# The last combination of a two-expert layer: every second pair of sequences moved from VectorE, ScalarE and GpSimd to TensorE

## What is computed

```python
x = x + jnp.tanh(g_xattn[0]) * _L0_xattn_ref(ctx_1024, ctx_1024, _layernorm(x, axis=-1), L0_xattn_w_out, L0_xattn_b_out)
x = x + jnp.tanh(g_ffn[0]) * _L0_ffn_ref(_layernorm(x, axis=-1), ...)
# the last lines of _L0_ffn_ref
ye = jnp.einsum('ecf,efd->ecd', h, W2) + b2[:, None, :]
out = ye[idx1, pos1] * (w1 * keep1)[:, None] + ye[idx2, pos2] * (w2 * keep2)[:, None]
```

## Time and profile before

| | before |
|---|---|
| median of 3 runs | 418.43 us (417.49 to 420.23) |
| the profiled execution, in all | 418.9 us |
| its span | 416.8 us |
| TensorE busy | 314.3 us (75%) |
| VectorE busy | 273.1 us (66%) |
| ScalarE busy | 220.2 us (53%) |
| GpSimd busy | 220.8 us (53%) |
| moved by DMA | 33.85 MB, mean 81 GB/s |

### The profile page before, as it was taken

How to read it: one execution, slowest core, us unless ns; L and a number is a source line. 1 busy time by engine, 2 the same in 40 slices (tenths; PEclk the granted TensorE clock), 3 DMA queues, 4 the chain that set the end, 5 groups by cost and what they waited for, 6 DMA issues and landing times.

```text
span 416.8 us, 13745 instructions
## 1 busy us (share of the span) xinstructions
PE 314.3 (75%) x3993; PEld 255.5 (61%) x3994; DVE 273.1 (66%) x1084; ACT 220.2 (53%) x656; POOL 220.8 (53%) x367
## 2 busy tenths in 40 slices
PE   1689987877878877878752079999999999999300
PEld 1356655545545545555441079999999998999300
DVE  4758987787787887876467425555555555555286
ACT  2478866665576566665430135555555555555131
POOL 2413366756656656656667105555555554555352
PEclk9999999999999999999995569999999999999755
DMA  7933321212212110000001212222222222221196
GB/s 204 304 113 108 114 90 65 78 40 77 76 43 80 61 57 29 21 28 29 25 29 47 71 44 64 64 64 63 63 64 65 63 67 56 61 60 56 55 355 197
DMA packets 40157, 33.85 MB, mean 81 GB/s; under 512 B 4998, under 2 KB 32936, under 8 KB 40112
## 3 DMA queue, kind: packets, MB, share of 16 engines
q1 hardware_dynamic: 35216, 24.58, 20.2%
q0 software_dynamic: 4320, 8.43, 6.3%
q10 hardware_dynamic: 576, 0.26, 0.3%
HBM read 17.95 MB, written 15.77 MB: 81 GB/s over the span
## 4 chain that ended last, share of the span: by engine, by line
PE 39%; issue 26%; ACT 13%; DVE 5%; DMA 4%; SPq 2%; another core or an unknown queue 1%; DVEq 1%; POOL 0%; ACTq 0%; POOLq 0%
PE main_scores L704 15%; PE main_scores L690 15%; ACT qT L520 5%; ACT probs L527 5%; PE max_scores L681 2%; DVE x_all L913 2%; DVE x_all L917 2%; PE main_scores L623 1%; DMA choice_rows<-y_s,dest 1%; PE mixed L598 1%; ACT oS L532 1%; DMA yc<-choice_rows 1%; ACT xn2T L512 1%; DMA expert_rows<-pad 1%
## 5 line engine op out<-in xcount | busy, mean ns | idle before, releaser
L474 POOL DMA_INDIRECT choice_rows<-y_s,dest x71 | 78.8, 1109 | 81.6 <-DVE y_s L894 46.5
L545 ACT ACTIVATE hT<-main_scores,ex_cur 128x128 f32<-128x128 f32 x284 | 81.2, 369 | 70.5 <-PE main_scores L690 69.7
L772 DVE TENSOR_REDUCE negmax<-max_scores 128x8 bf16<-128x1024 f32 x64 | 77.9, 1217 | 32.6 <-remote 21.7
L527 ACT ACTIVATE probs<-main_scores 128x1024 f32<-128x1024 f32 x64 | 62.0, 1021 | 45.7 <-issue 43.2
L690 PE MATMUL main_scores<-xtT,ex_cur 128*128 128x128 f32 x568 | 78.5, 282 | 1.5 <-DVE xtT L886 1.5
L704 PE MATMUL main_scores<-w_sb,hT 128*128 x568 | 79.2, 283 | 0.4 <-ACT hT L545 0.4
L431 POOL DMA_INDIRECT expert_rows<-xrow,slot_i x64 | 64.2, 1003 | 16.8 <-issue 16.1
L690 PEld LDWEIGHTS main_scores<-xtT,ex_cur 128*128 128x128 f32 x568 | 70.6, 195 | 3.3 <-DVE xtT L886 1.9
L704 PEld LDWEIGHTS main_scores<-w_sb,hT 128*128 128x128 f32 x568 | 69.6, 193 | 1.7 <-issue 0.6
L884 DVE COPY ex_cur<-ex_sb 128x644 f32 x71 | 35.3, 497 | 49.4 <-issue 35.4
L458 POOL TENSOR_TENSOR rstd<-ve,neg_half 128x1 f32<-128x1 f32 x32 | 17.7, 554 | 53.2 <-DVE ve L757 52.9
(11 more groups left out here) (132 smaller groups left out, 473.2 us busy)
## 6 DMA issues: line engine op xcount, KB each, us to landing
xt<-expert_rows SPq DMA_DIRECT2D x71, 64.5 KB
choice_rows<-zeros SPq DMA_DIRECT2D x16, 256.0 KB
yc<-choice_rows SPq DMA_DIRECT2D x16, 256.0 KB, 5.4
ex_sb<-in_L_ffn_W_dram SPq DMA_DIRECT2D x4, 512.0 KB, 4.7
w_sb<-in_L_ffn_W_dram SPq DMA_DIRECT2D x4, 512.0 KB, 4.4
out_dram<-x_all SPq DMA_DIRECT2D x8, 256.0 KB, 3.8
x_all<-in_x_dram SPq DMA_DIRECT2D x5, 384.0 KB, 6.2
ctx_all<-in_ctx_dram SPq DMA_DIRECT2D x5, 384.0 KB, 6.2
```

The source lines that it names most:

```text
L474: nc.gpsimd.indirect_dma_start(y_dram, bass.IndirectOffsetOnAxis(ap=dest[:, v, :], axis=0), y_s[:, v, :], None, bounds_check=last_row, oob ...
L527: nc.scalar.activation(probs[:, b % 2, 2 * g:2 * g + 2, :].rearrange("p g k -> p (g k)"), E_ALL[:, 1024 * g:1024 * g + 1024], ACT.Exp, sca ...
L545: last = nc.scalar.activation(hT[:, v % 2, c, :], H_BANK[v % 2][:, c * P:c * P + P], ACT.Gelu, bias=ex_cur[:, v, FF + D + c:FF + D + c + 1])
L772: V.tensor_reduce(negmax[:, m % 3, 2 * h:2 * h + 2, 0:J], S_ALL[:, :].rearrange("p (g j k) -> p g j k", g=2, j=J), AX.X, ALU.max, negate=T ...
```

## The change

In each chunk VectorE now takes two sequences instead of three (32 instructions instead of 48), and the other two go to TensorE. For each chunk TensorE adds up in one PSUM bank: x of both sequences (256 columns, times the identity), and for each of them its two answers, each multiplied by a 128x128 diagonal matrix with the gate of row s at place (s, s). ScalarE copies the 256 columns of the sum back into `x_all`. The 32 diagonal matrices (`diag`) are made by GpSimd from the identity and `gw`, after its last scatter to `expert_rows` and ahead of its first scatter to `choice_rows`. For that the six steps of `gw` move on VectorE from the end of stage 2 to its beginning. What ScalarE and GpSimd did in the last combination is gone.

```diff
+        diag = sb("diag", [P, K, B // 2, P])
...
             for k in range(NC):
-                sp.wait_ge(fin_done, (CH - 1) * (k + 1))
-                sp.wait_ge(pool_fin_done, k + 1)
+                sp.wait_ge(fin_done, CH // 2 * (k + 1))
+                sp.wait_ge(act_fin_done, k + 1)
...
+            pool.wait_ge(gates_done, 1)
+            for k in range(NC):
+                for c in range(K):
+                    for u in range(CH // 2):
+                        q = CH * k + CH // 2 + u
+                        last = nc.gpsimd.tensor_scalar(diag[:, c, CH // 2 * k + u, :], ident[:, :], gw[:, c, q:q + 1], None, ALU.mult)
+            last.then_inc(diag_done, 1)
             pool.wait_ge(zeroed, 16 * NZ)
...
-                    nc.gpsimd.tensor_tensor(x_all[:, cols(s)], x_all[:, cols(s)], yc[:, c, s, :],
-                                            ALU.add).then_inc(pool_fin_done if c else pool_first_added, 1)
...
-            act.wait_ge(gates_done, 1)
             for k in range(NC):
-                s = CH * k + CH - 1
-                act.wait_ge(yc_loaded[k], 16 * K)
-                for c in range(K):
-                    nc.scalar.activation(yc[:, c, s, :], yc[:, c, s, :], ACT.Copy, scale=gw[:, c, s:s + 1]).then_inc(scaled, 1)
+                s = CH * k + CH // 2
+                act.wait_ge(sum_psum, k + 1)
+                nc.scalar.copy(x_all[:, s * D:(s + CH // 2) * D], E_BANK[k % 4][:, 0:CH // 2 * D]).then_inc(act_fin_done, 1)
...
+            pe.wait_ge(diag_done, 1)
+            for v in (2, 3):
+                pe.wait_ge(y_ready[v], NI + (v < NV))
+            for k in range(NC):
+                s = CH * k + CH // 2
+                wait(pe, act_fin_done, k - 3)
+                nc.tensor.matmul(E_BANK[k % 4][:, 0:CH // 2 * D], ident[:, :], x_all[:, s * D:(s + CH // 2) * D],
+                                 start=True, stop=False, skip_group_check=True)
+                pe.wait_ge(yc_loaded[k], 16 * K)
+                for u in range(CH // 2):
+                    for c in range(K):
+                        last = nc.tensor.matmul(E_BANK[k % 4][:, u * D:u * D + D], diag[:, c, CH // 2 * k + u, :], yc[:, c, s + u, :],
+                                                start=False, stop=(c == K - 1), skip_group_check=True)
+                last.then_inc(sum_psum, 1)
...
-                mine = range(CH * k, CH * k + CH - 1)
+                mine = range(CH * k, CH * k + CH // 2)
```

More of the change, by code:

```diff
@@ L239, in flamingo_layer @@
         first_added, fin_done = sem("first_added"), sem("fin_done")
-        pool_first_added, pool_fin_done = sem("pool_first_added"), sem("pool_fin_done")
-        scaled = sem("scaled")
+        act_fin_done = sem("act_fin_done")
+        diag_done, sum_psum = sem("diag_done"), sem("sum_psum")
         stored = sem("stored")
@@ L481, in _ @@
                 scatter_tile(NI + 1, v)
-            for k in range(NC):
-                s = CH * k + CH - 1
-                for c in range(K):
-                    pool.wait_ge(scaled, K * k + c + 1)
-                    wait(pool, pool_first_added, c * (k + 1))
-                    nc.gpsimd.tensor_tensor(x_all[:, cols(s)], x_all[:, cols(s)], yc[:, c, s, :],
-                                            ALU.add).then_inc(pool_fin_done if c else pool_first_added, 1)
         @block.scalar
@@ L874, in _ @@
             V.tensor_scalar(row_tab[:, :], tile_r4[:, :], float(PAD_ROW), None, ALU.add).then_inc(table_done, 1)
+            dve.wait_ge(gexp_done, 1)
+            link(V.tensor_reduce(gsum[:, :], texp[:, :, :], AX.X, ALU.add))
+            link(V.tensor_scalar(gden[:, :], gsum[:, :], GATE_EPS, 1.0, ALU.mult, ALU.add))
+            link(V.tensor_tensor(gden2[:, :], gden[:, :], texp[:, :, 1], ALU.add))
+            link(V.reciprocal(grec[:, :], gden2[:, :]))
+            link(V.tensor_scalar(gw[:, 0, :], grec[:, :], tanh_g[:, 1:2], None, ALU.mult))
+            V.tensor_tensor(gw[:, 1, :], gw[:, 0, :], texp[:, :, 1], ALU.mult).then_inc(gates_done, 1)
             dve.wait_ge(moe_loaded, 16 * 9)
@@ L896, in _ @@
             tiles(dve, early, lambda i, v: None, back)
[L899 to L905, removed]
             dve.wait_ge(gates_done, 1)
@@ L915, in _ @@
                 for u, s in enumerate(mine):
-                    dve.wait_ge(first_added, (CH - 1) * k + u + 1)
+                    dve.wait_ge(first_added, CH // 2 * k + u + 1)
                     V.scalar_tensor_tensor(out=x_all[:, cols(s)], in0=yc[:, 1, s, :], scalar=gw[:, 1, s:s + 1], in1=x_all[:, cols(s)],
```

## The result

The changed kernel takes 426.19 us (median of 4, 425.86 to 428.05), the kernel before beside it 419.33 (4 runs): 1.0177 times as long, 95% interval 1.0125 to 1.0229. The forecast of 415.9 us and its range up to 420.5 were wrong. The span of the profiled execution is 423.6 us, against 416.8. That is 6.8 us, and it is a sum of two amounts of opposite sign.

The account below looks back on a forecast made before the run. VectorE was taken to bound the last 5.5 us. Span 416.8 - 2.6 (tail) + 0 (diagonals) = 414.2 us, 416.3 for the whole execution, 415.9 against the median; range 414.0 to 420.5.

Parts of the forecast that it names:

- Part 5: GpSimd's 32 diagonal matrices before the first scatter: 0.32 us a piece, 10.2 us in all, done at 247.5, loss 0.
- the threshold of 248.4: Start of the expert tiles: diagonals ending after 248.4, when y_s of tile 0 is done, cost nearly every microsecond in full.
- GpSimd's diagonals take too long: Rival at the first scatter: late diagonals eat the tail's gain; 0.13 for 1 to 2.6 us late, 0.15 later, 0.04 over 1%.
- The upper bound: GpSimd's dearest case per diagonal matrix: two-tile sum of 0.465 us, 0.578 crowded; 0.52 a piece, loss 5.5 us.
- The straight line through the copies: GpSimd copies of 64 and 2 columns extended to 128: 0.29 us; with something for the gate, 0.38 was taken.
- The estimate from the Trainium skill: One GpSimd diagonal multiplication: 192 ns for 128 elements plus 182 ns fixed, 0.37 us, also no loss.
- Part 2: TensorE in the tail: clock rises after 5.2 to 6 us, last sum at 410.5 instead of 413.4, gain 2.9 us.
- The rival of a clock that stays at half: TensorE in the tail never speeds up: last sum at 417.2, time 422.2 us; chance 0.08, half of it over 1%.
- so the clock decides: TensorE in the tail: a chunk takes 2.57 us at half clock, twice the loads' pace, or 1.34 at full, keeping pace.
- Part 1: VectorE in the tail: 32 passes instead of 48, following the loads, done at 409.0, 4.4 us earlier.
- Parts 3 and 4: ScalarE's eight tail copies of 0.38 us hidden except the last; gates moved before the expert tiles, ending 237.25, hidden.

Follow-up runs that it names:

- prices: Changed kernel with GpSimd's 32 diagonal multiplications replaced by four each of eight instruction kinds, to read their costs; one run, 424.70 us.
- warm: As split, plus 26 useless TensorE products before the answers of chunk 0 to keep its clock up; 0.9951 of the kernel before.
- split: Changed kernel, but GpSimd makes only the first gate's 16 diagonal matrices and ScalarE the second gate's 16; 0.9945 of the kernel before.
- nofourth: Kernel before without the fourth sequence's part of the last combination (ScalarE's scalings, GpSimd's sums), VectorE's 48 passes kept; 0.9931 of the kernel before.
- diag1: Changed kernel with one diagonal matrix made instead of 32 and used for every product (wrong gates); 0.994 of the kernel before.
- diag16: Changed kernel with only 16 diagonal matrices made, each used twice (wrong gates for half the products); 0.9916 of the kernel before.
- diag24: Changed kernel with only 24 diagonal matrices made (wrong gates for a quarter of the products); one run, 421.48 us.
- again: The changed kernel run once more, unaltered, beside other follow-up kernels; 1.016 of the kernel before.
- late: diag16 plus 36 plain GpSimd copies of a 128x128 tile that nothing reads, behind the 16 multiplications; 1.0137 of the kernel before.
- twotensors: Changed kernel with each diagonal matrix made as a product of two tensors, identity and broadcast gate; 0.9966 of the kernel before.
- The second group: Follow-up kernels run together, among them split, warm and nofourth, with their own runs of the kernel before.

## Why the prediction was wrong

**Part 5 failed: what a diagonal matrix costs GpSimd.** "No row shows GpSimd multiplying 128x128 by a column of scalars", it said, and took 0.32 us a piece between 0.18 and 0.52; measured was 19.83/32 = 0.62. Of the 9.6 us between 10.2 and 19.83 the undisturbed price makes 8.3 (0.58 a piece, 32 times). The other 1.3 are a term that the prediction put at nothing: "VectorE has little to do there, so I leave out the crowding". VectorE had only five copies of `ex_cur` to do in that time, and five matrices beside them took 0.23 to 0.32 us more each.

The mechanism was named as it happened: the first scatter, `dest` of tile 4 behind it, TensorE behind that, each microsecond paid nearly once (the matrices ended at 258.01, 9.6 us after the threshold of 248.4, and the last scatter came 9.25 us later). With 0.62 in the place of 0.32 the prediction's own sum gives 237.25 + 19.8 = 257.1, a loss of 8.7 us and 418.4 - 2.6 + 8.7 = 424.5; measured 426.2, beside a kernel before of 419.3. The rival "GpSimd's diagonals take too long" was the case that came true, with a chance of 0.04 for over 1%.

**The upper bound was no bound.** It came from a row of two operands (0.465) with crowding (0.578), on the argument that one operand must be cheaper than two. The prices show the reverse for this engine: 0.60 for the form with scalars against 0.396 for the product of two tiles. The straight line through the copies was right for copies (0.29 expected, 0.287 measured) and said nothing about another form. The profile of the kernel before had a warning that was not used: GpSimd's power of one column, L451, took 0.56 us for a single column, so an instruction's form can weigh more than its width.

The estimate from the Trainium skill (GPSIMD Engine Reference, section 3.1), 0.37 us, was too low as well: measured 0.60. Its section 4.1 puts one-input work at about the full rate; the copy's 0.287 agrees (VectorE copies 128 columns of `xtT` in 0.27 to 0.29), the multiplication by scalars does not. The measurement decides.

**Part 2 held.** The last sum was forecast for 410.5. Shifted by the 9.25 us of the stage before it, 419.75; measured 419.67 + 0.37 = 420.04. The clock: TensorE worked from 405.99 on at 0.50, and these windows of the changed kernel (columns as in rows 4) show the rise at about 412.2, 6.2 us later, where 5.2 to 6 was taken:

```profile
411.50:412.00 0.50, 0.50 (x4) 0.41 (x3) 0.34 (x3) 0.00 (x0) 0.00 (x0) 0.50 1.04 397
412.00:412.50 0.50, 0.50 (x5) 0.50 (x5) 0.50 (x4) 0.00 (x0) 0.00 (x0) 0.81 1.06 406
412.50:413.00 0.50, 0.50 (x6) 0.50 (x5) 0.31 (x2) 0.00 (x0) 0.00 (x0) 1.00 1.03 397
```

The rival of a clock that stays at half did not come. Yet "so the clock decides" was too strong: warm had the full clock from the start and was not faster than split.

**Part 1 held in its numbers, and not in its weight.** VectorE followed the loads and ended 1.1 us after the last chunk (417.25 to 418.39). The tail gave 2.4 us, forecast 2.6. But nofourth shows that the smaller number of passes was not needed for it.

**Parts 3 and 4 held.** ScalarE's copies are hidden but for the last; the gates ahead of the expert stage cost nothing (diag1 and diag16 keep them there and are faster than before the change). They ended at 238.08, not 237.25, because `texp` came that much later in this execution (at 236.26, not 235.39).

**The threshold** was put at 248.4, when `y_s` of tile 0 is done. The scatter started 0.17 us behind the last matrix, and the trace shows no wait for `y_s` before it, where it otherwise starts 0.86 us behind `y_s`. So about 0.7 us of lateness are free, as an estimate from these two gaps (that the queue had resolved its wait meanwhile is how they are read here; no run tests it). Against this, TensorE works at the half clock for a while after a stall: in diag24 from 257.45 to about 263, and its middle stretch is 1.1 us longer than that of the kernel before. In the five kernels in which TensorE stood still for 3.8 us or more (changed, again, late, prices and diag24) this stretch takes 141.95 to 143.34 us, in the others 140.74 to 141.65.

## What to carry to other kernels

Work that is moved into another engine's idle gap is free only up to the length of the gap, and behind it every microsecond may be paid in full: so the price of the moved instruction is worth a measurement of its own before anything else, with its own form, and not by a row of a form that looks harder. Where a row for it is missing, the honest upper end is the worst row of that engine, not the nearest; here that was 0.634 us, above the 0.60 that came. And where an engine is slowed by a neighbour, take the neighbour away first (nofourth): it gave here as much as the redistribution. A mean over four instructions of which two were disturbed is no price: look at the shortest ones too.

## What the hardware showed that was not expected

- On GpSimd a 128x128 float32 tile costs 0.60 us times a column of scalars, 0.52 times a constant, 0.39 times the same column broadcast as a second tensor, 0.39 as a sum with itself and 0.29 as a copy (undisturbed instructions of prices and twotensors).
- VectorE's passes beside GpSimd's sums took up to 0.6 us instead of 0.34, beside ScalarE's copies and TensorE's products 0.34 to 0.35 (the changed kernel, two in 0.61).
- It needs no two inputs: VectorE's copies of 644 columns took 0.50 to 0.68 us beside GpSimd's matrices in the changed kernel and 0.50 without them, and the matrices beside them 0.83 to 0.92 us instead of 0.60.
- The second group ran the kernel before in 388.4 us, the others in 419.3 and 417.5. By the record the second group ran on chip 5 and the other two on chip 13 (for the first result no chip is recorded). The difference lies ahead of the expert stage: the first scatter of split is at 219.55, that of diag16 at 248.46, and the stretch from first to last scatter is the same (140.74 and 141.28). ScalarE's exponentials take as long in both and idle far less before them, here first in diag16 (chip 13) and then in split (chip 5), columns as in rows 10:

```profile
L528 ACT ACTIVATE probs<-main_scores 128x1024 f32<-128x1024 f32 x64 | 62.0, 1021 | 45.3 <-issue 43.2 <-PE main_scores L627 2.0
```

```profile
L527 ACT ACTIVATE probs<-main_scores 128x1024 f32<-128x1024 f32 x64 | 62.0, 1021 | 8.5 <-issue 5.0 <-PE main_scores L632 2.5
```

  Why is not shown, nor that it is the chip and not something else of that group. It is a reason to compare only kernels that ran together.
